# One stream of NF4 chunks through the attention steps, value scaling on ScalarE, and loads and stores moved between queues

## The chip, the cores and the metric

The kernel runs on one core of a Trainium2 chip. The metric is the device time of one execution in microseconds (us); lower is better. Engine names in the profile: PE is TensorE (PEld its weight loads), DVE is VectorE, ACT is ScalarE, POOL is GpSimd, SP is SyncE, whose queue issues the DMAs.

## The reference, cut to what matters

```python
# 8 batches x 128 tokens x 512; 32 query heads in 8 key/value groups of 4, head size 128; hidden 1376
h  = layernorm(x)
q, k, v = h @ Wq, ctx @ Wk, ctx @ Wv ; q, k = rope(q), rope(k)
logits  = 30 * tanh(q k^T * 0.0884 / 30), masked ; weights = softmax(logits)
x = x + (weights @ v) @ Wo
d1, d2, d3 = nf4(w1), nf4(w2), nf4(w3)   # blocks of 64: divide by absmax, take the nearest of
                                         # 16 codes (15 thresholds), multiply by absmax again
h = layernorm(x)
x = x + (silu(h @ d1^T) * (h @ d2^T)) @ d3^T
```

## The kernel before, in words

Each engine has its own instruction list, written by hand and executed strictly in its order; engines meet only through semaphores (`wait_ge(name, value)`). Matrices are split into a high and a low part so that three matmuls in fp32r give about fp32 accuracy; ScalarE makes the high part, VectorE or GpSimd the low one.

- **Start** (to about 160 us): pieces of weights and context are loaded, K is projected in 16 units with rope, V in 16 units `v`, x is normalised, and the first six query units (of 64) are projected in between.
- **The 64 steps.** Step j = 8*kv + b (group kv, batch b) has one list per engine. TensorE: `weighted_values(j)`, query projection `q_unit(j+6)`, `logits(j+2)`, `transpose4` of `nrm` for j, `out_unit(j-1)` (projection with Wo). VectorE: `add_out(j-2)`, the reciprocal of the softmax sums `rs` (L1026), the scaling of the values into `nrm` (L1029), NF4 additions, `rope_parts(j+6)` (L898, reads the projection), the last NF4 addition, the low part `atl` of j (L1048). ScalarE: one NF4 comparison, `high` (a weight piece, L720), `weights(j+2)` (tanh L763, exp L765), the high part `ath` of j (L780), the remaining NF4 comparisons. GpSimd: low parts of weight pieces, `mask(j+2)` (L1215), `query_rope(j+6)` (L1149, after two DMAs `swap` that exchange halves through `sw`), and NF4 `nf_normalise` and `nf_rescale` (L1165).
- **NF4.** The weights w1, w2, w3 come as 12 chunks of 128 x 1408 (chunk 0 and 9 to 11 from w3). For one chunk: load, `nf_prepare` (absmax of blocks, L871 and two small ones), `nf_normalise`, then 15 pairs of a comparison on ScalarE (`nf_above_bound`, L702, into the two slots of `nfp`) and an addition on VectorE (`nf_add`, L887 and L890), then `nf_rescale` and a store to a scratch in memory. Chunk 0 is done in the start (15 pairs over v = 0 to 12), chunks 1 to 8 in the 64 steps, one for each group of 8 steps (mostly 2 pairs a step), chunks 9 to 11 in the feed-forward part.
- **Feed-forward** (from about 690 us): 22 hidden units, each 24 matmuls; then the 11 pieces of w3 are transposed and split, and the down projection runs to the end.

In VectorE's list, a step's additions are divided in this way, with `bounds` the list of the step's thresholds:

```python
before = max(1, len(bounds) - 1)
for i in bounds[:before]: nf_add(kv + 1, i)
...rope_parts...
for i in bounds[before:]: nf_add(kv + 1, i)
dve.wait_ge(at_hi, j + 1)            # then atl of step j
```

Of the kernel before, what the change touches and what calls it, by code (L numbers as in the profile page):

```python
# [5 lines left out]
B, S, D = 8, 128, 512  # L6
# [35 lines left out]
def build(nc, x_d, ctx_t, wk_d, wv_d, wq_d, wo_d, nf_d, mask_t, table_d, out_d):  # L42
# [5 lines left out]
    with ctx:  # L48
# [71 lines left out]
        with ExitStack() as loop:  # L120
            cs_loop = sb("cs_loop", [128, 2, 2, 512], f32, loop)
            nfx = sb("nfx", [128, CH], f32, loop)
# [67 lines left out]
        def nf_bufs(c):  # L190

            if c == 0:
                return nfv, nfa
            if c > NKV:
                return [(nfa, nfy), (nfv, nfa), (nfy, nfv)][c - NKV - 1]
            return NF_BUF[(2 * c - 4) % 3], NF_BUF[(2 * c - 3) % 3]
# [45 lines left out]
        def nf_values(v):  # L242

            return range(15 * v // 13, 15 * (v + 1) // 13) if v < 13 else range(0)
# [9 lines left out]
        def nf_head(kv, b):  # L254

            if kv == NKV - 1:
                return [[0, 1], [2, 3], [4, 5, 6], [7, 8], [9, 10], [11], [12], [13, 14]][b]
            return [[0, 1], [2, 3], [4, 5], [6, 7], [8, 9], [10, 11], [12], [13, 14]][b]
# [11 lines left out]
        def _(sp):  # L270
# [17 lines left out]
            def nf_load(c):  # L288
                if c == 1 or c == NKV + 1:
                    sp.wait_ge(nf_above, 15 * c)  # L290
                elif c > 1:
                    sp.wait_ge(nf_out, nf_stored(c - 2))
                sp.dma_start(nf_bufs(c)[0][:, :], nf_d[:, c * CH:(c + 1) * CH]).then_inc(nf_in, 16)
# [36 lines left out]
            sp.dma_start(y[:, :, :], x_d.rearrange("b s d -> s b d")).then_inc(x_in, 16)  # L330
            nf_load(0)
# [42 lines left out]
            def head(kv):  # L374
                last = kv == NKV - 1
                j = 8 * kv
                head_piece(j + 3)
                if kv > 0:
                    wait(sp, av_done, j)
                    sp.dma_start(vcur[:, 4:8, 0:DH], vs_d[kv, 1]).then_inc(v_in[1], 16)  # L380
                if kv > 0:
                    nf_store(kv)
                query_swap(j + AHEAD)
                head_piece(j + 4)
                query_swap(j + AHEAD + 1)
                if not last:
                    nf_load(kv + 2)
                if not last:
                    wait(sp, logits_done, j + 4)
                    sp.dma_start(kcur[:, 0, :], ks_d[kv + 1, 0]).then_inc(k_in[0], 16)  # L390
                head_piece(j + 5)
                query_swap(j + AHEAD + 2)
                head_piece(j + 6)
                query_swap(j + AHEAD + 3)
                head_piece(j + 7)
                if not last:
                    wait(sp, av_done, j + 4)
                    sp.dma_start(vcur[:, 0:4, 0:DH], vs_d[kv + 1, 0]).then_inc(v_in[0], 16)
                query_swap(j + AHEAD + 4)
                head_piece(j + 8)  # L400
                query_swap(j + AHEAD + 5)
                if not last:
                    wait(sp, logits_done, j + 8)
                    sp.dma_start(kcur[:, 1, :], ks_d[kv + 1, 1]).then_inc(k_in[1], 16)
                head_piece(j + 9)
                query_swap(j + AHEAD + 6)
                head_piece(j + 10)
                query_swap(j + AHEAD + 7)
                if last:
                    sp.wait_ge(nf_out, nf_stored(NKV - 1))  # L410
                    for n in range(4):
                        weights_in(n)
                    nf_load(NKV + 1)
# [15 lines left out]
            nf_store(NKV)  # L429
# [3 lines left out]
            nf_load(NKV + 2)  # L433
            for n in range(4, 2 * HT):
                if n == 15:
                    nf_store(NKV + 1)
                if n == 17:
                    nf_load(NKV + 3)
                weights_in(n)
            w3v = dq3[:, 0:4 * HID].rearrange("p (i h) -> p i h", i=4)  # L440
            for n in range(HT):
                m = 2 * HT + n
                cols = 128 if n < HT - 1 else HLAST
                if n in (2, 7):
                    nf_store(NKV + 2 + n // 7)
# [12 lines left out]
        def _(pe):  # L458
# [76 lines left out]

            for v in range(16):
# [10 lines left out]
                if u is not None:  # L547
                    pe.wait_ge(xt_lo, 8)
                    q_unit(u)

            def logits(j):

                kv, h, s = j // B, j % B // 4, j % 4
                if s == 0:
                    pe.wait_ge(roped, NK + 8 * kv + 4 * h + 4)
                    pe.wait_ge(k_in[h], 16 * kv + 16)
                wait(pe, tanh_done, j)
                nc.tensor.matmul(lgp[:, :], kcur[:, h, s * 128:(s + 1) * 128],  # L558
                                 qT[:, h, :, s * 128:(s + 1) * 128], start=True, stop=True).then_inc(logits_done, 1)
# [59 lines left out]
            logits(0)  # L619
# [75 lines left out]
        def _(act):  # L695
# [43 lines left out]
            for n in range(16):  # L739
                first_hi(n)  # L740
            for u in range(10, NK):
# [25 lines left out]
            def head(kv):  # L767
                last = kv == NKV - 1
                for b in range(B):
                    j = 8 * kv + b  # L770
                    bounds = nf_head(kv, b)
                    for i in bounds[0:1]:
                        nf_above_bound(kv + 1, i)
# [7 lines left out]
                    for i in bounds[1:]:  # L781
                        nf_above_bound(kv + 1, i)
# [9 lines left out]
            def weight_hi(n):  # L792
                act.wait_ge(wt_done, n + 1)
                if n >= 4:
# [29 lines left out]
            for n in range(len(UNITS)):  # L824
# [13 lines left out]
                for c, i in nf_ffn(n):  # L838
                    nf_above_bound(NKV + 1 + c, i)
            hidden_hi(2 * HT - 1)  # L840
            for c, i in nf_ffn(2 * HT):
                nf_above_bound(NKV + 1 + c, i)
# [12 lines left out]
        def _(dve):  # L855
# [22 lines left out]
            def nf_add(c, i):  # L878
# [3 lines left out]
                if i == 0:  # L882
                    if c == 1:
                        dve.wait_ge(vproj_done, 16)
                    if c == NKV + 1:
# [125 lines left out]
            nf_prepare(1)  # L1011
# [6 lines left out]
            def head(kv):  # L1018
                last = kv == NKV - 1
                for b in range(B):  # L1020
                    j = 8 * kv + b
                    if j > 1:
# [5 lines left out]
                    dve.wait_ge(recip_done, j + 1)  # L1028
                    nc.vector.tensor_tensor(  # L1029
                        nrm[:, b % 2, :].rearrange("p (a c d) -> p a c d", a=2, c=2),  # L1030
                        avp[:, :, 0:2 * (DH + 1)].rearrange("p a (c d) -> p a c d", c=2)[:, :, :, 0:DH],
                        rs[:, :].rearrange("p (a c o) -> p a c o", a=2, c=2).to_broadcast([128, 2, 2, DH]),
                        ALU.mult).then_inc(an_done, 1)

                    bounds = nf_head(kv, b)
                    before = max(1, len(bounds) - 1)
                    for i in bounds[:before]:
                        nf_add(kv + 1, i)
                    if b == 6 and not last:
                        nf_prepare(kv + 2)  # L1040
# [3 lines left out]
                    for i in bounds[before:]:  # L1044
# [252 lines left out]
```

## Time and profile before

| | |
|---|---|
| Time, median of 3 runs | 920.55 us (914.53 to 921.25) |
| The profiled execution: its own time | 916.73 us |
| Its span in the profile | 914.8 us |
| Mean granted TensorE clock | 0.962 of full speed |
| Busy: PE, DVE, ACT, POOL | 89%, 73%, 51%, 49% |

A row of the timeline reads: start in us, duration in us, engine, line, operation, output<-input with sizes, count, and in brackets the time for which the engine was idle before it and who released it. Neighbouring instructions of one engine overlap slightly in the record, so the distance from start to start is what counts in a sum.

### The profile page before, as it was taken

The page shows a single profiled execution, that of the slowest core. Times are in us where ns is not written, and L with a number is a line of the kernel's source. Part 1 is how long each engine was busy: PE and PEld are TensorE (multiplying, and loading weights), DVE is VectorE, ACT ScalarE, POOL GpSimd, SP SyncE. Part 2 cuts the span into 40 slices and gives each one's busy share as a digit, 9 for nine tenths or more (in the row PEclk, how much of TensorE's full clock was granted, in tenths as well). Part 3 has the DMA queues.
Part 4 walks back from the last instruction along what each step waited for, and adds up shares of the span by engine and source line. Part 5 has one row for each costly group of instructions (what it writes and reads, how often), then busy time and mean ns, then how long its engine had stood idle before and what let it go on. Part 6 is the DMA issues. An engine that isn't in the chain of part 4 may idle for free.

```text
span 914.8 us, 10681 instructions
## 1 busy us (share of the span) xinstructions
PE 818.3 (89%) x3806; PEld 650.5 (71%) x3806; DVE 669.7 (73%) x743; ACT 466.7 (51%) x571; POOL 446.3 (49%) x272
## 2 busy tenths in 40 slices
PE   6688893999999999999998998997779797994998
PEld 4576782677788777777886776775567686883886
DVE  3777752788888898888887987888766589698120
ACT  4014742565565656555655655655332576677100
POOL 1645056556857758659659568474102223253000
PEclk9899997999999999999999999999799999998999
DMA  9564735333433423435325234213013013120210
GB/s 328 151 188 140 209 92 169 90 81 93 144 92 90 126 79 114 123 81 155 81 70 167 58 92 144 57 48 101 1 32 133 24 35 114 32 76 23 84 58 35
DMA packets 63540, 91.75 MB, mean 100 GB/s; under 512 B 6784, under 2 KB 30464, under 8 KB 63488
## 3 DMA queue, kind: packets, MB, share of 16 engines
q1 hardware_dynamic: 63488, 91.07, 34.1%
q8 instruction: 31, 0.51, 0.2%
q14 instruction: 21, 0.17, 0.1%
HBM read 51.00 MB, written 19.07 MB: 77 GB/s over the span
## 4 chain that ended last, share of the span: by engine, by line
PE 51%; POOL 15%; DVE 13%; DMA 8%; issue 6%; ACT 5%; SPq 2%; POOLq 0%; DVEq 0%; ACTq 0%
POOL qT L1149 6%; PE bank L463 5%; PE bank L465 4%; PE bank L464 4%; DMA sw<-cs_loop 4%; PE bank L558 4%; PE bank L497 3%; PE bank L499 3%; PE bank L498 3%; PE bank L481 3%; PE bank L482 3%; PE bank L483 3%; PE avp L569 3%; DMA sw<-cs_start 3%; PE trp L470 2%
## 5 line engine op out<-in xcount | busy, mean ns | idle before, releaser
L1149 POOL TENSOR_TENSOR qT<-cs_loop,sw 128x512 f32<-128x512 f32 x58 | 92.6, 1597 | 104.9 <-DMA sw<-cs_loop 99.8
L763 ACT ACTIVATE eb<-bank 128x512 f32<-128x512 f32 x64 | 38.3, 598 | 194.4 <-PE bank L558 194.4
L890 DVE SCALAR_TENSOR_TENSOR nfa<-nfp,nfa 128x1408 f32<-128x1408 uint8 x56 | 106.8, 1907 | 32.5 <-ACT nfp L702 31.2
L890 DVE SCALAR_TENSOR_TENSOR nfv<-nfp,nfv 128x1408 f32<-128x1408 uint8 x56 | 106.5, 1902 | 28.0 <-ACT nfp L702 26.8
L1215 POOL TENSOR_TENSOR eb<-eb,maskf 128x512 f32<-128x512 f32 x64 | 91.1, 1425 | 62.4 <-ACT eb L765 62.4
L702 ACT ACTIVATE nfp<-nfv,bnd 128x1408 uint8<-128x1408 f32 x75 | 107.0, 1460 | 20.4 <-POOL nfv L1165 15.8
L497 PE MATMUL bank<-woh,ath 128*128 128x512 f32 x256 | 109.4, 427 | 0.0
L481 PE MATMUL bank<-xh,wqh 128*128 128x512 f32 x256 | 106.5, 416 | 0.0
L499 PE MATMUL bank<-woh,atl 128*128 128x512 f32 x256 | 103.2, 403 | 0.0
L498 PE MATMUL bank<-wol,ath 128*128 128x512 f32 x256 | 103.0, 402 | 0.0
L890 DVE SCALAR_TENSOR_TENSOR nfx<-nfp,nfx 128x1408 f32<-128x1408 uint8 x42 | 79.9, 1902 | 30.2 <-ACT nfp L702 30.2
L483 PE MATMUL bank<-xh,wql 128*128 128x512 f32 x256 | 101.5, 397 | 0.0
L482 PE MATMUL bank<-xl,wqh 128*128 128x512 f32 x256 | 101.5, 396 | 0.0
L702 ACT ACTIVATE nfp<-nfa,bnd 128x1408 uint8<-128x1408 f32 x60 | 85.2, 1460 | 8.6 <-POOL nfa L1165 5.6
L1250 POOL TENSOR_TENSOR hl<-hf,hh 128x512 fp32r<-128x512 f32 x22 | 33.8, 1536 | 96.7 <-ACT hh L812 96.7
L569 PEld LDWEIGHTS avp<-vcur,eb 128*128 128x128 f32 x512 | 67.3, 193 | 18.9 <-POOL eb L1215 14.4
L569 PE MATMUL avp<-vcur,eb 128*128 128x129 f32 x512 | 68.4, 277 | 13.6 <-POOL eb L1215 13.6
L558 PE MATMUL bank<-qT,kcur 128*128 128x512 f32 x128 | 66.4, 600 | 13.2 <-POOL qT L1149 12.5
L470 PEld LDWEIGHTS trp<-tab,nrm 128*128 128x128 f32 x288 | 35.3, 144 | 57.2 <-DVE nrm L1029 31.5
L898 DVE TENSOR_TENSOR cs_loop<-bank,csq 128x1024 f32<-128x1024 f32 x58 | 69.9, 1206 | 2.0 <-PE bank L483 2.0
L463 PE MATMUL bank<-xh,wgh 128*128 128x512 f32 x176 | 71.2, 404 | 0.0
L464 PE MATMUL bank<-xl,wgh 128*128 128x512 f32 x176 | 69.8, 397 | 0.0
(134 smaller groups left out, 1814.4 us busy)
## 6 DMA issues: line engine op xcount, KB each, us to landing
sw<-cs_loop SPq DMA_DIRECT2D x116, 128.0 KB, 2.3
stage<-wq_pieces SPq DMA_DIRECT2D x32, 256.0 KB, 2.9
stage<-wo_pieces SPq DMA_DIRECT2D x32, 256.0 KB, 2.9
stage<-dq_scratch SPq DMA_DIRECT2D x32, 256.0 KB, 3.2
sw<-cs_start SPq DMA_DIRECT2D x44, 128.0 KB, 2.4
ks_scratch<-qT SPq DMA_DIRECT2D x16, 256.0 KB, 2.3
vs_scratch<-vst SPq DMA_DIRECT2D x16, 256.0 KB, 3.3
kcur<-ks_scratch SPq DMA_DIRECT2D x16, 256.0 KB, 3.2
```

The source lines that it names most:

```text
L463: nc.tensor.matmul(out, wh, mh, start=i == 0, stop=False)
L464: nc.tensor.matmul(out, wh, ml, start=False, stop=False)
L481: nc.tensor.matmul(o, wqh[:, g, k, :], xh[:, k, cs], start=k == 0, stop=False)
L482: nc.tensor.matmul(o, wqh[:, g, k, :], xl[:, k, cs], start=False, stop=False)
L483: last = nc.tensor.matmul(o, wql[:, g, k, :], xh[:, k, cs], start=False, stop=k == KT - 1)
L497: nc.tensor.matmul(o, ah, wh[:, g, :], start=g == 0, stop=False)
L498: nc.tensor.matmul(o, ah, wl[:, g, :], start=False, stop=False)
L499: last = nc.tensor.matmul(o, al, wh[:, g, :], start=False, stop=g == G - 1)
L569: av = nc.tensor.matmul(avp[:, g // 2, (g % 2) * (DH + 1):(g % 2 + 1) * (DH + 1)], eb[:, b % 2, g * 128:(g + 1) * 128], vcur[:, b, :], sta ...
L702: nc.scalar.activation(nfp[:, n % 2, :], nf_bufs(c)[0][:, :], ACT.Sign, bias=bnd[:, i:i + 1])\
L890: op = nc.vector.scalar_tensor_tensor(acc[:, :], nfp[:, n % 2, :], STEPS[i], acc[:, :], ALU.mult, ALU.add)
L1149: nc.gpsimd.tensor_tensor(dst, products(ru, slot)[:, 0, :], sw[:, slot, :], ALU.add).then_inc(roped, 1)
```

## The change

- The chunks 1 to 9 form one stream of positions, 16 for a chunk (15 pairs and, at the 13th position, the preparation of the next chunk). Steps 0 to 55 take 33 positions per 14 steps, steps 56 to 63 take 12 in 8. So a step has 1, 2 or 3 pairs. Chunk 9 moves from the feed-forward part into the steps; chunks 10 and 11 stay there, at 2 positions for each hidden unit, from unit 1 to unit 16. The buffers of the chunks are renamed accordingly.
- The scaling of the values into `nrm` leaves VectorE and becomes four ScalarE activations (one per head, 128 columns each, scale from `rs`). They stand first in ScalarE's list of a step, behind a wait for this step's reciprocal.
- x is loaded from ScalarE's queue after its 10th piece, chunk 0 after its 16th. Chunk 0's 15 pairs are spread over v = 0 to 10.
- `nf_store(0)` moves behind the last exchange of the start; in the steps, stores and loads of chunks stand behind the exchanges; SyncE's list of a step is written as a loop. `logits(0)` moves ahead of the sixth query unit; GpSimd normalises chunk 1 and masks step 0 ahead of its sixth rope.

```diff
         def nf_values(v):
-            return range(15 * v // 13, 15 * (v + 1) // 13) if v < 13 else range(0)
+            return range(15 * v // 11, 15 * (v + 1) // 11) if v < 11 else range(0)
+        def nf_sequence(lo, hi, first):
+            steps = [(first + p // 16, p % 16) for p in range(lo, hi)]
+            adds = [(c, r if r < 12 else r - 1) for c, r in steps if r != 12]
+            return adds, [c + 1 for c, r in steps if r == 12], [c for c, r in steps if r == 15]
+        def nf_head(j):
+            lo, hi = [33 * i // 14 if i <= 56 else 132 + 12 * (i - 56) // 8 for i in (j, j + 1)]
+            return nf_sequence(lo, hi, 1) if 0 <= j < NSTEP else ([], [], [])
         def nf_ffn(n):
-            return [divmod(k, 15) for k in range(45 * (n - 2) // 21, 45 * (n - 1) // 21)] if n >= 2 else []
+            lo, hi = [2 * (i - 1) for i in (n, n + 1)]
+            return nf_sequence(max(0, lo), min(hi, 32), NKV + 2)
@@ sync, start @@
-            sp.dma_start(y[:, :, :], x_d.rearrange("b s d -> s b d")).then_inc(x_in, 16)
-            nf_load(0)
...
-                if v == 13:
+                if v == 12:
                     nf_load(1)
-                if v == 14:
-                    nf_store(0)
...
+            nf_store(0)
             for i in range(4):
                 wait(sp, v_out[i], 64)
@@ sync, feed-forward @@
             for n in range(4, 2 * HT):
-                if n == 15:
-                    nf_store(NKV + 1)
-                if n == 17:
+                if n == 6:
                     nf_load(NKV + 3)
+                if n == 18:
+                    nf_store(NKV + 2)
                 weights_in(n)
@@ tensor, start @@
                 if u is not None:
                     pe.wait_ge(xt_lo, 8)
+                    if v == 15:
+                        logits(0)
                     q_unit(u)
@@ scalar, start @@
             for n in range(16):
                 first_hi(n)
+                if n == 9:
+                    act.dma_start(y[:, :, :], x_d.rearrange("b s d -> s b d")).then_inc(x_in, 16)
+            act.dma_start(nfv[:, :], nf_d[:, 0:CH]).then_inc(nf_in, 16)
@@ scalar, a step @@
-                    bounds = nf_head(kv, b)
-                    for i in bounds[0:1]:
-                        nf_above_bound(kv + 1, i)
+                    act.wait_ge(recip_done, j + 1)
+                    for g in range(G):
+                        col = (g % 2) * (DH + 1)
+                        last_part = nc.scalar.activation(nrm[:, b % 2, g * DH:(g + 1) * DH],
+                                                         avp[:, g // 2, col:col + DH], ACT.Copy, scale=rs[:, g:g + 1])
+                    last_part.then_inc(an_done, 1)
+                    adds = nf_head(j)[0]
+                    for c, i in adds[0:1]:
+                        nf_above_bound(c, i)
                     if not last:
                         high(32 + j)
...
                     nc.scalar.activation(ath[:, j % 4, :], trp[:, :], ACT.Copy).then_inc(at_hi, 1)
-                    for i in bounds[1:]:
-                        nf_above_bound(kv + 1, i)
+                    for c, i in adds[1:]:
+                        nf_above_bound(c, i)
@@ vector, a step @@
-                    dve.wait_ge(recip_done, j + 1)
-                    nc.vector.tensor_tensor(
-                        nrm[:, b % 2, :].rearrange("p (a c d) -> p a c d", a=2, c=2),
-                        avp[:, :, 0:2 * (DH + 1)].rearrange("p a (c d) -> p a c d", c=2)[:, :, :, 0:DH],
-                        rs[:, :].rearrange("p (a c o) -> p a c o", a=2, c=2).to_broadcast([128, 2, 2, DH]),
-                        ALU.mult).then_inc(an_done, 1)
-
-                    bounds = nf_head(kv, b)
-                    before = max(1, len(bounds) - 1)
-                    for i in bounds[:before]:
-                        nf_add(kv + 1, i)
-                    if b == 6 and not last:
-                        nf_prepare(kv + 2)
+                    adds, prepares, _ = nf_head(j)
+                    before = max(1, len(adds) - 1)
+                    for c, i in adds[:before]:
+                        nf_add(c, i)
+                    for c in prepares:
+                        nf_prepare(c)
                     u = j + AHEAD
                     if u < NUNIT:
                         rope_parts(NK + u, u % 2, csq[:, :, :])
-                    for i in bounds[before:]:
-                        nf_add(kv + 1, i)
+                    for c, i in adds[before:]:
+                        nf_add(c, i)
@@ gpsimd, start @@
+            for u in range(AHEAD):
+                if u == 5:
+                    nf_normalise(1)
+                    mask(0)
+                query_rope(u)
+                if u in (1, 3):
+                    for n in (28 + u - 1, 29 + u - 1):
+                        low(n % 4, woh0[:, n % 4, :], wol0[:, n % 4, :], n)
+                if u == 1:
+                    nf_rescale(0)
+            mask(1)
```

## Rows read from the trace of the kernel before

**Rows 1.** The page, part 1: busy us, share of the span, instructions, by engine.

```profile
PE 818.3 (89%) x3806; PEld 650.5 (71%) x3806; DVE 669.7 (73%) x743; ACT 466.7 (51%) x571; POOL 446.3 (49%) x272
```

**Rows 2.** Stage table, 250 to 300 us: busy PE, PEld, DVE, ACT, POOL; clock.

```profile
250.00:300.00 50.00, 49.96 (x244) 39.33 (x243) 42.99 (x49) 30.21 (x39) 32.43 (x20) 1.00 0.34 94
```

**Rows 3.** Timeline of VectorE, step 55, up to the reciprocal of step 56.

```profile
603.19 0.17 DVE L1026 RECIPROCAL rs<-avp 128x4 f32<-128x4 f32 x1
...
605.54 1.22 DVE L898 TENSOR_TENSOR cs_loop<-bank,csq 128x1024 f32<-128x1024 f32 x1
608.82 1.94 DVE L890 SCALAR_TENSOR_TENSOR nfx<-nfp,nfx 128x1408 f32<-128x1408 uint8 x1 [2.07 <-ACT nfp L702]
610.68 0.68 DVE L1048 TENSOR_TENSOR atl<-trp,ath 128x512 fp32r<-128x512 f32 x1
...
611.88 0.17 DVE L1026 RECIPROCAL rs<-avp 128x4 f32<-128x4 f32 x1
```

**Rows 4.** Timeline of ScalarE in the same step.

```profile
605.68 0.60 ACT L763 ACTIVATE eb<-bank 128x512 f32<-128x512 f32 x1 [4.10 <-PE bank L558]
...
607.33 1.46 ACT L702 ACTIVATE nfp<-nfv,bnd 128x1408 uint8<-128x1408 f32 x1
```

**Rows 5.** Timeline of ScalarE in step 1, its list without gaps.

```profile
166.96 2.82 ACT L702 ACTIVATE nfp<-nfv,bnd 128x1408 uint8<-128x1408 f32 x2
169.68 0.62 ACT L720 ACTIVATE wqh<-stage 128x512 fp32r<-128x512 f32 x1
170.30 0.60 ACT L763 ACTIVATE eb<-bank 128x512 f32<-128x512 f32 x1
```

**Rows 6.** Timeline of VectorE, step 58, the only one with three pairs.

```profile
627.60 0.17 DVE L1026 RECIPROCAL rs<-avp 128x4 f32<-128x4 f32 x1
...
632.39 3.35 DVE L890 SCALAR_TENSOR_TENSOR nfv<-nfp,nfv 128x1408 f32<-128x1408 uint8 x2 [2.37 <-ACT nfp L702]
...
636.87 0.17 DVE L1026 RECIPROCAL rs<-avp 128x4 f32<-128x4 f32 x1
```

**Rows 7.** Groups by line and form: busy us, mean ns, idle before.

```profile
L720 ACT ACTIVATE wqh<-stage 128x512 fp32r<-128x512 f32 x28 | 17.3, 619 | 0.0
...
L1029 DVE TENSOR_TENSOR nrm<-avp,rs 128x512 f32<-128x512 f32 x64 | 44.2, 691 | 2.2
...
L890 DVE SCALAR_TENSOR_TENSOR nfx<-nfp,nfx 128x1408 f32<-128x1408 uint8 x42 | 79.9, 1902 | 30.2 <-ACT nfp L702 30.2
```

**Rows 8.** Timeline of VectorE: preparation of a chunk, to the next instruction.

```profile
745.82 1.61 DVE L871 TENSOR_REDUCE nfm<-nfv 128x22 f32<-128x1408 f32 x1
...
747.89 3.29 DVE L890 SCALAR_TENSOR_TENSOR nfy<-nfp,nfy 128x1408 f32<-128x1408 uint8 x2
```

**Rows 9.** Timeline of VectorE, reciprocal of step 0.

```profile
160.75 0.18 DVE L1026 RECIPROCAL rs<-avp 128x4 f32<-128x4 f32 x1 [14.30 <-PE avp L569]
```

**Rows 10.** Timelines of GpSimd and of SyncE's queue, end of the start.

```profile
139.81 1.28 POOL L1149 TENSOR_TENSOR qT<-cs_start,sw 128x512 f32<-128x512 f32 x1 [3.52 <-DMA sw<-cs_start]
141.05 2.53 POOL L1140 TENSOR_TENSOR wol<-stage,woh 128x512 fp32r<-128x512 f32 x2
...
146.11 0.88 SPq L303 DMA_DIRECT2D dq_scratch<-nfa  x2
...
154.80 2.55 POOL L1165 TENSOR_TENSOR nfv<-nfv,nfr 128x1408 f32<-128x1408 f32 x1
157.31 2.49 POOL L1215 TENSOR_TENSOR eb<-eb,maskf 128x512 f32<-128x512 f32 x2
```

**Rows 11.** Timeline of TensorE, a K unit of the start after a wait.

```profile
27.85 0.77 PE L523 MATMUL bank<-cth,wch 128*128 128x512 f32 x1 [5.60 <-DVE cs_start L898]
```

**Rows 12.** TensorE's waits in the feed-forward part: us in total, times, longest.

```profile
PE bank L671 <- DVE w3l L1125: 11.7, 1, 11.7
PE bank L470 <- DMA stage<-dq_scratch: 5.0, 1, 5.0
PE trp L470 <- DVE wgl L1072: 4.9, 1, 4.9
```

More of the change, by code:

```diff
@@ L375, in head @@
                 last = kv == NKV - 1
[L376 to L413, printed above, removed]
+                for b in range(B):
+                    j = 8 * kv + b
+                    head_piece(j + 3)
+                    if b == 0 and kv > 0:
+                        wait(sp, av_done, j)
+                        sp.dma_start(vcur[:, 4:8, 0:DH], vs_d[kv, 1]).then_inc(v_in[1], 16)
+                    if b == 4 and not last:
+                        wait(sp, av_done, j)
+                        sp.dma_start(vcur[:, 0:4, 0:DH], vs_d[kv + 1, 0]).then_inc(v_in[0], 16)
+                    query_swap(j + AHEAD)
+                    if b in (1, 5) and not last:
+                        wait(sp, logits_done, j + 3)
+                        sp.dma_start(kcur[:, b // 4, :], ks_d[kv + 1, b // 4]).then_inc(k_in[b // 4], 16)
+                    for c in nf_head(j - 2)[2]:
+                        nf_store(c)
+                    for c in nf_head(j - 3)[2]:
+                        nf_load(c + 2)
+                    if j == 1:
+                        nf_load(2)
+                    if last and b == 3:
+                        sp.wait_ge(nf_out, nf_stored(NKV - 1))
+                        for n in range(4):
+                            weights_in(n)
@@ L534, in _, with logits @@
                     first_transposes(u - 10)
+            def logits(j):
+                kv, h, s = j // B, j % B // 4, j % 4
+                if s == 0:
+                    pe.wait_ge(roped, NK + 8 * kv + 4 * h + 4)
+                    pe.wait_ge(k_in[h], 16 * kv + 16)
+                wait(pe, tanh_done, j)
+                nc.tensor.matmul(lgp[:, :], kcur[:, h, s * 128:(s + 1) * 128],
+                                 qT[:, h, :, s * 128:(s + 1) * 128], start=True, stop=True).then_inc(logits_done, 1)
             for v in range(16):
@@ L1112, in _ @@
                 hidden(n)
-                if n in (1, 7, 14):
-                    nf_prepare(NKV + 1 + n // 7)
-                for c, i in nf_ffn(n):
-                    nf_add(NKV + 1 + c, i)
-            for c, i in nf_ffn(2 * HT):
-                nf_add(NKV + 1 + c, i)
+                adds, prepares, _ = nf_ffn(n)
+                for c in prepares:
+                    if c < 12:
+                        nf_prepare(c)
+                for c, i in adds:
+                    nf_add(c, i)
             for n in range(HT):
@@ L1200, in query_rope @@
                 rope(NK + u, u % 2, qT[:, half, g, :])
-            for u in range(AHEAD):
-                query_rope(u)
-                if u in (1, 3):
-                    for n in (28 + u - 1, 29 + u - 1):
-                        low(n % 4, woh0[:, n % 4, :], wol0[:, n % 4, :], n)
-                if u == 3:
-                    nf_rescale(0)
-            nf_normalise(1)
             def mask(j):
@@ L1222, in head @@
                     j, slot = 8 * kv + b, b % 4
-                    if b == 7 and not last:
-                        nf_normalise(kv + 2)
-                    if b == 0 and kv > 0:
-                        nf_rescale(kv)
+                    for c in nf_head(j - 1)[2]:
+                        nf_rescale(c)
                     if not last and b < 4:
@@ L1234, in head @@
                         query_rope(j + AHEAD)
+                    for c in nf_head(j)[1]:
+                        nf_normalise(c)
                     if last and b == 4:
@@ L1238, in head @@
                         power(2, range(2, 4))
-            mask(0)
-            mask(1)
             for kv in range(NKV):
```

57 lines of the change are left out of this document (22 added, 35 removed).

## The prediction

> **What bounds the kernel now.** I read the page's busy shares first: TensorE is busy for 89% of the span, VectorE for 73%, ScalarE for 51% [rows 1]. By these numbers ScalarE has room for more work. But a share is a mean over stages, so I went to the table of stages: in a 50 us stretch of the 64 steps TensorE is busy for 49.96 us, VectorE for 42.99, ScalarE for 30.21 [rows 2]. From the reciprocal of step 0 at 160.75 [rows 9] to that of step 56 at 611.88 [rows 3] are 451.1 us, 8.06 us a step. TensorE is the bound there, with VectorE a little below it.
>
> Then I looked at which wait ends last for VectorE within a step, because its list and ScalarE's refer to each other. In step 55 the reciprocal starts at 603.19, the last NF4 addition at 608.82 after 2.07 us of waiting for ScalarE's comparison, `atl` follows 1.86 us later, and 1.20 us after that (`atl` and `add_out`, 0.60 each) the next reciprocal [rows 3]. ScalarE started its tanh at 605.68, released by TensorE's logits, and the comparison that VectorE waited for at 607.33 [rows 4]. So before the change the chain inside a step starts at TensorE: logits, tanh, exp, `ath`, comparison, addition, `atl`, `add_out`, reciprocal. Nothing in ScalarE's list waits for the reciprocal itself; it depends on it only through TensorE's transposes.
>
> **The steps: a closed ring between two engines.** The change puts the four scaling activations at the head of ScalarE's step, behind a wait for the reciprocal. Queued behind that wait are a comparison, `high`, tanh, exp, `ath` and the other comparisons; VectorE waits for the last of these before its last addition, and only then come `atl`, `add_out` and the next reciprocal. That is a ring: reciprocal of j, ScalarE's step up to the comparison that the last addition needs, the end of VectorE's step, reciprocal of j+1. No buffer loosens it, since both lists are in order. Its length, start to start:
> - reciprocal to ScalarE: 0.17 and 0.03 of handing over (comparison at 607.33 ends at 608.79, addition starts at 608.82 [rows 3, 4]): 0.20.
> - four activations of 128 columns. No row shows one that narrow. The comparison over 1408 columns takes 1.46 [rows 4], the copy over 512 takes 0.62 [rows 7]: 0.94 ns a column and 0.14 fixed, so 0.26 each, 1.05 for four. Bounds: 0.5 (the columns alone) and 1.9 (each at about the 0.48 by which a 512-wide one advances its engine, if the fixed part of one that reads PSUM and a scale were as large as that). I take 1.05, as both rows lie on that line.
> - first comparison: two in a row take 2.82, so 1.36; `high` to tanh 0.62 [rows 5].
> - tanh to the last addition's start: 608.82 - 605.68 = 3.14 [rows 3, 4].
> - addition to `atl`: 1.86 in step 55; two additions in a row take 3.35 in step 58, so 1.6 at least [rows 3, 6], 1.54 with the overlap; the mean duration is 1.90 [rows 7].
> - `atl` and `add_out`: 1.20.
>
> For a step with two pairs: 0.20+1.05+1.36+0.62+3.14 = 6.37 to the last addition, then 1.54 to 1.86, then 1.20: 9.1 to 9.4 us. A check: in step 55 the same addition started 5.63 after the reciprocal, and the step took 8.69; 0.74 later gives 9.43.
>
> For three pairs VectorE does two before `rope_parts`, and the second of these needs a comparison that ScalarE makes behind `ath`. So `rope_parts` (1.14 [rows 3]) and one more addition go onto the ring: 11.8 to 12.4. Step 58, the one with three pairs now, took 9.27 without rope, its second addition starting at 4.79 [rows 6]; 6.37 - 4.79 + 1.14 later is 12.0.
>
> The preparation of a chunk (2.07 [rows 8]) lies between the first addition and `rope_parts`. First addition at 2.74, then 1.54 to 1.86, 2.07, 1.14: 7.5 to 7.8, past the 6.37. With two pairs 10.2 to 10.9, with one 8.7 to 9.0.
>
> Steps 0 to 55 by the new rule: 33 with two pairs, 15 with three, 5 with two and a preparation, 3 with one and a preparation. The sum is 555 with the short additions and 579 with the long ones. The mean of the additions speaks for the long ones, less traffic of GpSimd for the short ones; I take 572, against 451: +121. What VectorE sheds (0.69 a step [rows 7]) does not shorten the ring; it is replaced by 1.05 on ScalarE plus 1.36 and 0.62 which were beside it before. TensorE needs 8.06 a step and waits for the scaled values; its projections still run beside the ring.
>
> Steps 56 to 63: they have 11 additions where there were 15, 7.6 us less by the mean, no `high`, and the first steps of the feed-forward part between them, which were already serial. Against it stand the ring in the three steps with two pairs and the preparation in step 61. I put the difference at 0, with 6 either way.
>
> The Trainium skill, ScalarE: Activation LUTs, section What ACT_TABLE_LOAD costs, gives 280 ns + 0.833 ns a column for an activation with one pointer operand, and an overlap of 93 ns; the comparison here agrees (1453 against 1460 ns), and four of 128 columns would come to about 1.27 by it, an estimate that adds 12 us over 56 steps. The same page, section Rules for kernel authors, sends multiplications to VectorE; by the rows here the move costs 1.05 against 0.69 in busy time alone, and the ring is worth much more than that.
>
> **The start.** x and chunk 0 leave SyncE's queue, where the first exchange stood behind them. TensorE waited 5.60 us at 27.85 for that [rows 11]; I count 4 of it as gained (0 to 6, since the same 16 DMA engines carry x either way). Issuing the two DMAs costs ScalarE 0 to 2 us, hidden as its next work then is the first transpose of x, long after. Chunk 0's pairs in 11 instead of 13 steps `v` put about one pair more on a ScalarE that TensorE already waits for there: 1 us lost (0 to 3).
>
> At the end of the start GpSimd's last rope came late, as its exchange was queued behind the store at 146.11, which waited for the rescaling; then came the normalisation at 154.80 and the mask at 157.31 [rows 10], and TensorE began the steps. Now: rope 3 at 139.81 to 141.1, two low parts (2.5), rope 4 (1.3), normalisation (2.5), first mask (1.3) end at 148.7 instead of 158.6: 9.9 gained. All of the start: -13, between -18 and -7. The logits ahead of the sixth query unit cost TensorE up to a microsecond of waiting for rope 3, within that.
>
> **The feed-forward part.** Three waits of TensorE [rows 12]. 4.9 us: the low parts of weights stood behind an addition that waited for chunk 9's normalisation; that chunk is now done in the steps and chunk 10 is prepared there. 5.0: a weight piece behind a store in SyncE's queue; the store now comes at n = 18, when its data have long been ready. 11.7: the splitting of w3 behind the last additions; these end at unit 16 of 22, and a serial transpose, high and low part of about 2.5 remain. Gain 19, and about 1 for the slow clock after the waits (the matmul after the 5.60 us wait takes 0.77 [rows 11], and its line's mean is about half of that): -20, bounds -14 and -26.
>
> **Sum.** 914.8 - 13 + 121 + 0 - 20 = 1003 of span; with the 1.9 that lie around it (916.73 - 914.8) 1005. That execution is 0.4% under the median of 920.55, which is no more than the runs spread; I leave it so.
>
> **The rivals.**
> - Faster: the sum of loads decides and the ring does not bind. VectorE's 6.9 us a step (42.99/50 x 8.06 [rows 2]) stay 6.8 (0.69 less, and 2.2 additions instead of 1.9), ScalarE's 4.9 become 6.4 (1.05, and 0.3 comparisons), TensorE stays the bound, and the better placed exchanges save some 5 us of its waits. 914.8 - 13 - 20 - 5 + 1.9 = 879. It holds if ScalarE's wait for the reciprocal ends less than about 2 us after TensorE's values, so early that the ring is under 8.06. Against it: the ring's members are all rows, in list order, and even its shortest form with activations of 0.5 us gives 8.6. 8%.
> - About the same: the ring binds only in the steps with three pairs, which costs 15 x 4 = 60 less what short steps give back, so that it nearly pays for the gains: 915 to 945. For it: steps with one pair are shorter than TensorE's work. Against it: there are 3 of these in 56. 5%.
> - Much slower, by the clock: TensorE waits 1 to 4 us in each step, and falls to the lower of its levels (1.2 of 2.4 GHz) as it did at 27.85 [rows 11]. At the lower level for half of the time its step would be 8.06 x 1.5 = 12.1, more than the ring, 678 for 56 steps: 1110. Against it: its chain from the reciprocal to the next values skips the query projection, so that it can lose 1 to 2 us a step unseen. 7%.
> - Slower by dear activations: 1.9 for four puts 0.85 on 64 steps: 1059. 10%.
> - The forecast: 70%.
>
> The range: from cheap activations and short additions (-29 and -17, start and end at their good bounds -11, not all at once) to dear ones: 960 to 1050. A measurement of this kernel tells about 1% from no change. Faster by more: 8%, with a little of the second rival 9%; within 1%: 2%; slower: 89%.
>
> **What would show it.** Right: the distance of reciprocals is 9 to 9.5 in most steps and about 12 in those with three pairs; ScalarE's idle time stands before the first scaling activation, released by VectorE's reciprocal, about 3 us a step; TensorE's transposes wait for `nrm` from ScalarE in nearly every step; the mask of step 0 ends near 149; no wait of over 4 us in TensorE's feed-forward part. Wrong: TensorE busy for over 95% between 200 and 600 us, or its clock there under 0.9.

## The result and the profile after

The changed kernel takes 1009.79 us (median of 4 runs, 1007.07 to 1011.64) against 917.54 for the kernel before: 1.100 times, interval 1.094 to 1.1065. It is 10% slower. The forecast was 1005 in 960 to 1050.

Busy shares, from the page of the kernel after (compare [rows 1]):

```profile
PE 857.4 (85%) x3806; PEld 671.8 (67%) x3806; DVE 629.0 (62%) x679; ACT 532.4 (53%) x827; POOL 444.4 (44%) x272
```

No engine is over 85%, and none of the other three is over 62%. A table of loads finds no bound here. The stage table, of the same columns as [rows 2], says it again for a stretch of the steps:

```profile
300.00:350.00 50.00, 43.57 (x200) 33.94 (x199) 32.86 (x32) 31.19 (x52) 24.37 (x16) 0.94 0.34 93
```

What ended the idle times does find it. The waits of ScalarE and of VectorE over the whole span, in the kernel after:

```profile
ACT nrm L765 <- DVE rs L1024: 242.2, 64, 5.7
```

```profile
DVE nfa L887 <- ACT nfp L690: 73.8, 40, 2.6
DVE nfv L887 <- ACT nfp L690: 71.6, 38, 2.6
DVE nfx L887 <- ACT nfp L690: 69.8, 35, 5.2
```

ScalarE waits 242 us for the reciprocal, in each of the 64 steps, and VectorE 215 us for ScalarE's comparisons. Two engines that wait for each other in step after step, while both are busy for less than two thirds of the time, look like a ring; the experiments below test it. The timeline of VectorE in one step with two pairs and one with three (compare [rows 3] and [rows 6]; L1024 is the reciprocal, L895 `rope_parts`, L1040 `atl`, L1013 `add_out`):

```profile
306.74 0.17 DVE L1024 RECIPROCAL rs<-avp 128x4 f32<-128x4 f32 x1
309.47 1.63 DVE L887 SCALAR_TENSOR_TENSOR nfa<-nfp,nfa 128x1408 f32<-128x1408 uint8 x1 [2.56 <-ACT nfp L690]
311.01 1.22 DVE L895 TENSOR_TENSOR cs_loop<-bank,csq 128x1024 f32<-128x1024 f32 x1
312.98 2.00 DVE L887 SCALAR_TENSOR_TENSOR nfa<-nfp,nfa 128x1408 f32<-128x1408 uint8 x1 [0.75 <-ACT nfp L690]
314.91 0.68 DVE L1040 TENSOR_TENSOR atl<-trp,ath 128x512 fp32r<-128x512 f32 x1
...
316.11 0.17 DVE L1024 RECIPROCAL rs<-avp 128x4 f32<-128x4 f32 x1
...
322.35 1.99 DVE L887 SCALAR_TENSOR_TENSOR nfa<-nfp,nfa 128x1408 f32<-128x1408 uint8 x1 [1.89 <-ACT nfp L690]
324.27 1.21 DVE L895 TENSOR_TENSOR cs_loop<-bank,csq 128x1024 f32<-128x1024 f32 x1
325.40 1.61 DVE L887 SCALAR_TENSOR_TENSOR nfa<-nfp,nfa 128x1408 f32<-128x1408 uint8 x1
...
328.13 0.17 DVE L1024 RECIPROCAL rs<-avp 128x4 f32<-128x4 f32 x1
```

And ScalarE in the first of these steps (compare [rows 4, 5]; L765 scaling, L690 comparison, L708 `high`, L754 tanh, L756 exp, L777 `ath`):

```profile
306.94 1.14 ACT L765 ACTIVATE nrm<-avp,rs 128x128 f32<-128x128 f32 x4 [3.93 <-DVE rs L1024]
307.95 1.48 ACT L690 ACTIVATE nfp<-nfx,bnd 128x1408 uint8<-128x1408 f32 x1
309.31 0.64 ACT L708 ACTIVATE woh<-stage 128x512 fp32r<-128x512 f32 x1
309.83 0.61 ACT L754 ACTIVATE eb<-bank 128x512 f32<-128x512 f32 x1
310.48 0.63 ACT L756 ACTIVATE eb<-eb 128x512 f32<-128x512 f32 x1
311.01 0.58 ACT L777 ACTIVATE ath<-trp 128x512 fp32r<-128x512 f32 x1
311.49 1.46 ACT L690 ACTIVATE nfp<-nfx,bnd 128x1408 uint8<-128x1408 f32 x1
```

Read it from 306.74: reciprocal, at 306.94 ScalarE wakes, runs through its list without one gap, at 312.98 VectorE's last addition can start, and at 316.11 comes the next reciprocal: 9.37 us. In the second step `rope_parts` has come to stand between two additions: 12.02 us.

The reciprocals of steps 0 and 56, at 160.75 and 611.88 before, are now at 148.15 and 730.37. So the start gained 12.6 us, steps 0 to 55 lost 131.1 (582.2 against 451.1), and the rest, 302.9 before and 278.5 now, gained 24.4. Their sum, +94.1, is the difference of the spans (1008.9 - 914.8).

### The profile page after: what moved, and what is told of

The parts are those of the page before. It is cut to its first block, busy times and chain, and to the rows that moved or that the text cites. A ratio compares the mean times of both kernels' runs of the same rounds, so it can differ in the third digit from the quotient of the medians.

```text
span 1008.9 us, 10873 instructions
## 1 busy us (share of the span) xinstructions
PE 857.4 (85%) x3806; PEld 671.8 (67%) x3806; DVE 629.0 (62%) x679; ACT 532.4 (53%) x827; POOL 444.4 (44%) x272
## 4 chain that ended last, share of the span: by engine, by line
PE 32%; ACT 24%; DVE 22%; issue 15%; DMA 4%; POOL 2%; SPq 1%; ACTq 0%; POOLq 0%; DVEq 0%
ACT nfp L690 13%; ACT nrm L765 5%; PE bank L450 4%; PE bank L452 4%; PE bank L451 4%; DVE nfa L887 4%; DVE y L1013 3%; DVE nfx L887 3%; DVE nfv L887 3%; ACT ath L777 2%; ACT eb L754 2%; PE bank L659 2%; PE bank L660 2%; PE bank L661 2%; DVE cs_loop L895 2%
## 5 line engine op out<-in xcount | busy, mean ns | idle before, releaser
L765 ACT ACTIVATE nrm<-avp,rs 128x128 f32<-128x128 f32 x256 | 73.0, 368 | 242.2 <-DVE rs L1024 242.2
L887 DVE SCALAR_TENSOR_TENSOR nfa<-nfp,nfa 128x1408 f32<-128x1408 uint8 x56 | 101.8, 1818 | 74.5 <-ACT nfp L690 73.8
L1141 POOL TENSOR_TENSOR qT<-cs_loop,sw 128x512 f32<-128x512 f32 x58 | 74.0, 1276 | 164.0 <-DMA sw<-cs_loop 164.0
L484 PE MATMUL bank<-woh,ath 128*128 128x512 f32 x256 | 123.2, 481 | 0.0
L457 PE MATMUL trp<-tab,nrm 128*128 128x128 f32 x288 | 53.6, 317 | 79.9 <-ACT nrm L765 79.7
L485 PE MATMUL bank<-wol,ath 128*128 128x512 f32 x256 | 114.3, 446 | 0.0
L486 PE MATMUL bank<-woh,atl 128*128 128x512 f32 x256 | 112.9, 441 | 0.0
L690 ACT ACTIVATE nfp<-nfv,bnd 128x1408 uint8<-128x1408 f32 x75 | 108.6, 1466 | 3.8 <-POOL nfv L1157 3.0
L530 PE MATMUL bank<-qT,kcur 128*128 128x512 f32 x128 | 72.4, 649 | 35.4 <-POOL qT L1141 35.2
L1132 POOL TENSOR_TENSOR wol<-stage,woh 128x512 fp32r<-128x512 f32 x32 | 70.5, 2207 | 41.6 <-ACT woh L708 41.6
L1132 POOL TENSOR_TENSOR wql<-stage,wqh 128x512 fp32r<-128x512 f32 x28 | 62.3, 2225 | 59.2 <-ACT wqh L708 59.2
L690 ACT ACTIVATE nfp<-nfa,bnd 128x1408 uint8<-128x1408 f32 x60 | 86.9, 1467 | 1.2 <-POOL nfa L1157 1.0
L895 DVE TENSOR_TENSOR cs_loop<-bank,csq 128x1024 f32<-128x1024 f32 x58 | 70.0, 1207 | 0.0
```

What stands on the lines that cost most here:

```text
L457: last = nc.tensor.transpose(out[0:p, i * 128:(i + 1) * 128], src(i), tab[:, 2, :])
L484: nc.tensor.matmul(o, ah, wh[:, g, :], start=g == 0, stop=False)
L485: nc.tensor.matmul(o, ah, wl[:, g, :], start=False, stop=False)
L486: last = nc.tensor.matmul(o, al, wh[:, g, :], start=False, stop=g == G - 1)
L690: nc.scalar.activation(nfp[:, n % 2, :], nf_bufs(c)[0][:, :], ACT.Sign, bias=bnd[:, i:i + 1])\
L765: last_part = nc.scalar.activation(nrm[:, b % 2, g * DH:(g + 1) * DH], avp[:, g // 2, col:col + DH], ACT.Copy, scale=rs[:, g:g + 1])
```

## The experiments

Each run is compared with the kernel before, measured again beside it (medians of 916 to 918). The first ones ask whether it is the ring, and whether its members have the prices that the forecast gave them.

**The scaling back on VectorE.** Everything else of the change stays. The first hunk is ScalarE's step, the second VectorE's, behind the reciprocal.

```diff
@@ scalar @@
-                    act.wait_ge(recip_done, j + 1)
-...
@@ vector @@
+                    dve.wait_ge(recip_done, j + 1)
+                    nc.vector.tensor_tensor(
+...
+                        ALU.mult).then_inc(an_done, 1)
```

> The changed kernel with the scaling of the values back on VectorE as one instruction behind the reciprocal; all else of the change stays. Ring theory: ScalarE's list no longer waits for the reciprocal, the steps with two pairs fall from 9.7 back to about 8.1 us, those with three from 12.0 to about 10, with a preparation to about 8.8; 56 steps in about 485 to 500 instead of 582, time 910 to 930. Load theory (the slowdown comes from more work on ScalarE and lower TensorE clock in proportion): VectorE is given 44 us more, ScalarE 73 less, time 990 to 1010. Chunk theory (the ninth chunk in the steps is what costs): no change, about 1009.

Measured: 935.6 us, ratio to before 1.020 (1.017 to 1.023). 74 of the 92 us are gone with the ring, though VectorE is given work and its busy time rises from 629 to 674. The load theory and the theory that the ninth chunk alone is the cost fall. It is 6 us above the range: steps with three pairs take 11.2, not 10, and the 56 steps 513 where 485 to 500 were expected and the kernel before takes 451. So the rest of the change, the stream of chunks above all, has a price of its own in the steps, with no ring between the two engines.

**The scaling on ScalarE, but third in its list.** The same instructions, in another order.

```diff
+                    adds = nf_head(j)[0]
+                    for c, i in adds[0:1]:
+                        nf_above_bound(c, i)
+                    if not last:
+                        high(32 + j)
                     act.wait_ge(recip_done, j + 1)
...
-                    adds = nf_head(j)[0]
-                    for c, i in adds[0:1]:
-                        nf_above_bound(c, i)
-                    if not last:
-                        high(32 + j)
```

> The changed kernel with the same instructions, but in ScalarE's list of a step the wait for the reciprocal and the four scaling activations stand behind the first comparison and the copy high, ahead of tanh. Ring theory: these two (1.36 + 0.52) leave the ring, which is then 0.20+1.05+3.14+1.86+1.20 = 7.4 us for two pairs, below TensorE's 8.06, and 10.3 for three; 56 steps in 490 to 510, time 915 to 940. Load theory: the work of each engine is unchanged, so about 1009. Chunk theory: about 1009.

Measured: 944.6 us, 1.029 (1.022 to 1.035). No engine's work changed and 65 us went, by order alone. The range is missed by 5 us: the steps with three pairs take 11.2 and not 10.3, the ones with two 8.6 in the mean, 7.95 in the median.

**One member off the ring.**

```diff
-                    if not last:
-                        high(32 + j)
                     if j + 2 < NSTEP:
                         weights(j + 2)
...
                     for c, i in adds[1:]:
                         nf_above_bound(c, i)
+                    if not last:
+                        high(32 + j)
```

> The changed kernel with only the copy high moved behind the last comparison of a step. Ring theory: 0.52 us leave the ring in 56 steps, -29 us, time 975 to 985, unless the later low parts on GpSimd delay the rope (then up to 1000). Load theory and chunk theory: about 1009.

Measured: 984.2 us, 1.074 (1.070 to 1.077), 25.5 less than the changed kernel. The copy advances ScalarE by 0.52 (309.31 to 309.83 above), 29 us in 56 steps, and the 56 steps fell by 23.4, from 582.2 to 558.8. The price of 0.52 is not seen by itself in every kind of step. The median step with two pairs fell by 0.89, from 9.36 to 8.47, since the last addition got shorter too; start to start to `atl` it is 1.54 here and was 1.93 above (312.98 to 314.91):

```profile
300.59 1.63 DVE L887 SCALAR_TENSOR_TENSOR nfa<-nfp,nfa 128x1408 f32<-128x1408 uint8 x1 [0.23 <-ACT nfp L690]
302.13 0.68 DVE L1040 TENSOR_TENSOR atl<-trp,ath 128x512 fp32r<-128x512 f32 x1
```

Step 0 fell by 4.1, while the steps with three pairs kept their mean of 12.06 (their median fell by 0.47). So the sum comes near the forecast in part by balance.

**The scaling alone, on the kernel before.** The activations head ScalarE's step, and VectorE's multiplication into nrm is taken out.

```diff
+                    act.wait_ge(recip_done, j + 1)
+...
                     bounds = nf_head(kv, b)
```

> The kernel before with one part of the change alone: the four scaling activations at the head of ScalarE's step behind the wait for the reciprocal, instead of VectorE's instruction. Ring theory: the steps of two pairs take 9.3 to 9.5 instead of 8.06, 56 steps in about 525 instead of 451, time 985 to 1000. Load theory: VectorE sheds 44 us and ScalarE stays under 65% busy, about 917 or less. Chunk theory: no change, 917.

Measured: 1000.6 us, 1.091 (1.087 to 1.095), 0.6 above the range. With 1.9 pairs a step and none of the new chunk stream, 56 steps take 527.5 (451.1 before). Every one is nearly alike: reciprocal to reciprocal 9.29 to 9.75. So this one edit carries most of the loss. The rest of the change adds 9 us on top of it. That is a balance and not nothing: in the spans these 56 steps get 55 us longer with the chunk stream in them (582.2 against 527.5), and the start gives back 12 and the part behind step 56 another 32.

**`rope_parts` off the ring,** in the steps with three pairs.

```diff
-                    before = max(1, len(adds) - 1)
+                    before = 1
```

> The changed kernel with VectorE doing only the first addition of a step ahead of rope_parts (so in steps with three pairs the second one comes behind it). Ring theory: in these 15 steps rope_parts (1.14) leaves the ring, 12.0 falls to 10.9, -17 us, and with exchanges that start 3 us earlier TensorE's logits wait less; 990 to 995. The rival that the steps with three pairs cost because of VectorE's load: no change, about 1009.

Measured: 992.9 us, 1.083 (1.080 to 1.086). Timeline of VectorE in such a step of this run:

```profile
308.00 0.17 DVE L1024 RECIPROCAL rs<-avp 128x4 f32<-128x4 f32 x1
...
312.27 1.22 DVE L895 TENSOR_TENSOR cs_loop<-bank,csq 128x1024 f32<-128x1024 f32 x1
314.24 3.73 DVE L887 SCALAR_TENSOR_TENSOR nfa<-nfp,nfa 128x1408 f32<-128x1408 uint8 x2 [0.75 <-ACT nfp L690]
...
319.09 0.17 DVE L1024 RECIPROCAL rs<-avp 128x4 f32<-128x4 f32 x1
```

11.09 where it was 12.02: `rope_parts` now lies in VectorE's wait for the comparison. The 1.13 by which it advances VectorE are gone, and the two additions behind it take 0.2 more than in the changed kernel. So `rope_parts` was on the ring at the price that the term for three pairs gave it.

**The same edit with the scaling on VectorE** (x1 and x5 together).

> The run with the scaling back on VectorE, and rope_parts ahead of the second addition as in x5. Without the ring the open chain from TensorE's logits over ScalarE to the last additions still holds in steps with three pairs (11.2 there). Chain theory: rope_parts leaves it, 11.2 falls to about 9.8, 56 steps from 513 to about 492, time 912 to 918. Load theory (VectorE now has 2.2 additions and the scaling, 7.6 us a step): the time stays at 935.

Measured: 911.9 us, 0.996 (0.993 to 1.000), at the lower end of the range. 24 us less than x1; steps with three pairs 10.1, 56 steps in 490.9. This is as fast as the kernel before, with one chunk more in the steps: the start and the feed-forward part now pay for the loop.

**Two comparisons ahead.** With the scaling on VectorE (the first run) and with it on ScalarE behind the two comparisons and `high` (the second). Both also have the edit of x5, `before = 1`.

```diff
-                    for c, i in adds[0:1]:
+                    for c, i in adds[0:2]:
                         nf_above_bound(c, i)
...
-                    for c, i in adds[1:]:
+                    for c, i in adds[2:]:
                         nf_above_bound(c, i)
```

> As x6 (scaling on VectorE), and ScalarE does two comparisons of a step ahead of high and tanh, where it waits for logits anyway. Chain theory: in steps with two pairs nothing of NF4 lies behind ath, in those with three only one pair; VectorE's own 7.6 us and TensorE's 8.06 decide, 56 steps in 455 to 470 instead of 513, time 875 to 895. Load theory: 935.

> As x8, but with the scaling on ScalarE as in x2: two comparisons, high, then the wait for the reciprocal and the four activations, then tanh. The ring is 0.20+1.05+0.63+0.54+0.60+1.20 = 4.2 for two pairs and about 8 for three, so TensorE decides; VectorE has 6.8 us a step instead of 7.6. Chain theory: 56 steps in 450 to 465, time 870 to 890, at or below x8. Rival: the move to ScalarE is bad by itself (four activations of 1.05 against 0.69): 10 us or more above x8.

Measured: 891.7 us, 0.973 (0.9705 to 0.975), and 891.9, 0.9725 (0.970 to 0.975). Both beat both kernels. 56 steps took 476 and 473 us, 6 and 8 over the forecasts, and the second run's time is 2 us above its range. The move to ScalarE is not bad by itself: tanh, exp and `ath` still wait behind it, but the ring that is left, 4.2 us for two pairs by the expectation, is far below TensorE's step, and the two runs are alike. In the second, two steps took over 14 us. ScalarE's timeline in one of them:

```profile
307.27 1.46 ACT L690 ACTIVATE nfp<-nfx,bnd 128x1408 uint8<-128x1408 f32 x1
315.74 1.47 ACT L690 ACTIVATE nfp<-nfv,bnd 128x1408 uint8<-128x1408 f32 x1 [7.00 <-POOL nfv L1157]
317.11 0.61 ACT L708 ACTIVATE woh<-stage 128x512 fp32r<-128x512 f32 x1
317.63 1.12 ACT L770 ACTIVATE nrm<-avp,rs 128x128 f32<-128x128 f32 x4
```

The comparison that was drawn forward is the first of a new chunk; it waits for GpSimd's normalisation, with the scaling, tanh and exp queued behind it. It is the fault of the change again, in small.

**Not across a chunk's start.** For both places of the scaling, on top of the last two runs.

```diff
+                    ahead = 1 if len(adds) > 1 and adds[1][1] == 0 else 2
-                    for c, i in adds[0:2]:
+                    for c, i in adds[0:ahead]:
                         nf_above_bound(c, i)
...
-                    for c, i in adds[2:]:
+                    for c, i in adds[ahead:]:
                         nf_above_bound(c, i)
```

> As x9, but where the second comparison of a step is the first of a new chunk, ScalarE does it behind ath again and not ahead of tanh. In x9 two of the steps of this kind (20 and 54) took 14.3 and 14.2 us. Chain theory: ScalarE stood there waiting for GpSimd's normalisation with tanh and the scaling queued behind it; they fall to about 8, 10 to 13 us in all, time 878 to 883. Rival: the long steps come from somewhere else (a late weight piece or rope), then 890 as x9.

> As x8 (scaling on VectorE) with the same edit. Its steps of this kind took 10.4 and 10.0, so about 2 us each are to be had: 886 to 890. If the scaling on ScalarE is worth its place once it is off the ring, because VectorE is next to the bound, x11 ends 5 us or more below this run; if the two engines are both covered by TensorE, within 2.

Measured: 885.6 us, 0.964 (0.959 to 0.970), and 886.6, 0.967 (0.962 to 0.9725). In the first run the two long steps fell from 14.3 and 14.2 to 9.2 and 8.9. In the second, where they were 10.4 and 10.0, they fell by 0.5 and 0.6 and not by the 2 expected, so they explain only 1 of the 5 us that it gained over x8. The time is 3 us above the forecast for the first. The difference of the two runs, 1 us, is within the bound set for "both covered". The better one is the fastest kernel of the study, 3.6% under the kernel before.

**Two comparisons ahead, on the kernel before.**

```diff
-                    for i in bounds[0:1]:
+                    for i in bounds[0:2]:
                         nf_above_bound(kv + 1, i)
...
-                    for i in bounds[1:]:
+                    for i in bounds[2:]:
                         nf_above_bound(kv + 1, i)
```

> The kernel before with one edit only: ScalarE does two comparisons of a step ahead of high and tanh. With 1.9 pairs a step TensorE was the bound there and VectorE waited 2 us a step for a comparison without harm. Chain theory: the loop stays at TensorE's 8.06, at best its waits for the rope (about 10 us) go: 907 to 917. Rival: what made x8 fast is the order of the comparisons alone, not the better start and feed-forward part: about 892.

Measured: 903.4 us, 0.986 (0.980 to 0.993), 4 us under the range of the chain theory and 11 above the rival's 892. The steps went from 451.1 to 443.4. The reciprocals come 7.74 apart in most of the steps (the median step of the kernel before took 7.75 already), and VectorE waits for TensorE at both ends of a step, as its timeline shows:

```profile
307.80 0.18 DVE L1026 RECIPROCAL rs<-avp 128x4 f32<-128x4 f32 x1 [0.20 <-PE avp L569]
...
314.65 0.69 DVE L1015 TENSOR_TENSOR y<-bank,y 128x512 f32<-128x512 f32 x1 [0.69 <-PE bank L499]
315.54 0.18 DVE L1026 RECIPROCAL rs<-avp 128x4 f32<-128x4 f32 x1 [0.20 <-PE avp L569]
```

So 7.74 is TensorE's own step (it was busy for 50.00 of the 50 us from 250 to 300), and the 8.06 that the prediction called TensorE's need was too high. Of the 0.32 between them this order took back 0.14; TensorE's waits for the rope, 9.3 us in 6 waits between 162 and 600, are most of the rest. Of what x11 gains over the kernel before (32 us), this order alone has 14. The rest is a balance: x11's start and its part behind step 56 are 10.5 and 26 us shorter than here, and its 56 steps, with the ninth chunk in them, 21 longer.

The steps 0 to 55 by kind, mean distance of the reciprocals in us, worked out from the timeline of each run's profiled execution (that of x2 took 936.0, 8.6 less than its median; the others are within 3.5 us of theirs):

| run | two pairs | three pairs | two, preparation | one, preparation | sum of 56 |
|---|---|---|---|---|---|
| before | 8.16 | | | 7.30 | 451.1 |
| forecast | 9.1 to 9.4 | 11.8 to 12.4 | 10.2 to 10.9 | 8.7 to 9.0 | 572 |
| after | 9.68 | 12.05 | 10.84 | 9.30 | 582.2 |
| x4, scaling alone | 9.44 | | | 9.30 | 527.5 |
| x3, high last | 9.11 | 12.06 | 10.20 | 8.72 | 558.8 |
| x5, rope first | 9.41 | 11.35 | 10.84 | 9.30 | 562.9 |
| x2, scaling third | 8.58 | 11.15 | 8.81 | 7.17 | 516.0 |
| x1, scaling back | 8.38 | 11.19 | 8.92 | 8.07 | 513.3 |
| x6 | 8.24 | 10.11 | 8.80 | 7.73 | 490.9 |
| x8 | 7.61 | 10.46 | 8.90 | 7.89 | 476.3 |
| x9 | 7.71 | 10.09 | 8.90 | 7.51 | 472.7 |
| x11 | 7.43 | 10.24 | 8.67 | 7.51 | 464.8 |
| x12 | 7.65 | 10.10 | 8.93 | 7.76 | 471.7 |
| x13 | 7.94 | | | 7.74 | 443.4 |

## Why the prediction was right, point by point

**The ring** was right in its mechanism (x1, x2: off the ring most of the loss goes, with the same work or more) and in its members (x3, x4, x5: `high` 0.52, the scaling with what it drags behind it 76 us on the kernel before, `rope_parts` 1.13). Their sizes were near and their errors offset each other. The four activations advance ScalarE by 1.01 us (306.94 to 307.95) where 1.05 was taken, `high` by 0.52 where 0.62 was, so that the last addition starts 6.24 after the reciprocal where 6.37 was; the addition itself takes 1.93 to `atl`, above the 1.54 to 1.86 of the forecast.

**The steps' sum** was 10 us short, 131 for 121. The median step with two pairs is 9.36, within its bounds; the mean of 9.68 is not. Most of the difference lies in seven of the 33 steps with two pairs. Step 0 took 13.0, as ScalarE waited for a weight piece whose load had moved behind the chunk's store:

```profile
154.44 0.63 ACT L708 ACTIVATE wqh<-stage 128x512 fp32r<-128x512 f32 x1 [3.57 <-DMA stage<-wq_pieces]
```

The load's place does that, and not the ring: in x1, without the ring, step 0 takes 12.7 with the same wait. The other six (6, 14, 26, 34, 42 and 54) took 9.7 to 11.4. Each stands behind a step with a late `rope_parts`, and is one in which TensorE's logits need that rope. They waited for it for 4 to 5.8 us, of which 0.6 to 1.3 came through to ScalarE's tanh. In TensorE's waits of the kernel after:

```profile
PE trp L457 <- ACT nrm L765: 79.7, 31, 5.8
PE bank L530 <- POOL qT L1141: 35.2, 10, 5.8
```

Before, the wait for the rope was 12.5 us. The prediction put `rope_parts` on the ring and did not ask who else was waiting for it. x5 agrees: its steps with two pairs fall from 9.68 to 9.41, though the edit does not touch them. Step 14, behind one with three pairs, fell from 11.38 to 9.01, and step 6, behind a preparation that x5 leaves as it was, stayed at 10.6; a quarter of the fall is its step 0, 10.8 for 13.0. The wait is not the whole of it, as longer additions beside GpSimd's normalisation take part too. This one is in step 6:

```profile
214.81 2.89 DVE L887 SCALAR_TENSOR_TENSOR nfx<-nfp,nfx 128x1408 f32<-128x1408 uint8 x1 [2.56 <-ACT nfp L690]
```

TensorE's transposes waited for `nrm` 31 times and their weight loads 46 times, not in nearly every one of the 64 steps as foreseen. ScalarE's wait for the reciprocal is 3.8 us a step where about 3 was.

**The start** was right in its sum, 12.6 for 13, and not in its parts. The mask of step 0 ends at 146.9, 11.7 us sooner, where 9.9 was worked out, since rope 3 itself came 3 us sooner, at 136.70 for 139.81; in SyncE's queue a chunk's load stood just ahead of its exchange before and does not now, which fits, though no run tests it. The exchanges that start sooner at the front of the kernel gave nothing in the end: TensorE's wait of 5.60 at 27.85 became two of 2 us, and `rope_parts` of the third K unit came 4.0 us sooner (22.47 for 26.48), but that of the eighth only 1.4 and that of the sixteenth 0.3. A wait for a context piece, before and after, stayed nearly as it was:

```profile
PE bank L523 <- DVE ctl L914: 6.3, 1, 6.3
PE bank L510 <- DVE ctl L911: 5.9, 1, 5.9
```

The 4 us counted there did not come through: the copy of the last V unit stands at 140.37 where it stood at 139.61. So the whole gain of the start was made behind that point, and that the sum of 13 came out is luck in these terms.

**The last eight steps and the feed-forward part** gained 24.4 for 20. Of TensorE's three waits [rows 12] that of 5.0 is gone, of that of 4.9 some 1.2 is left, and that of 11.7 is this:

```profile
PE bank L659 <- DVE w3l L1117: 2.4, 1, 2.4
```

2.5 had been left for it. The other 4 us are within the 6 given to steps 56 to 63; no run here parts them. In the sum of the forecast they stand against the 10 missed in the steps, which brings 1005 within 5 us of 1009.8.

**The rivals.** The sum of loads failed: no engine was full. "About the same" failed, as every kind of step got longer, those with one pair too (9.3). The clock did fall, from a mean of 0.962 to 0.932, and in stretches of 50 us between 200 and 750 it was 0.88 to 0.97; one of the two signs given for "wrong", a clock under 0.9, was touched in single stretches, while the mean of 200 to 600 is 0.92. In the typical step it was hidden as argued: x4, at a mean clock of 0.962, has a median of 9.37 in its steps with two pairs, and the changed kernel at 0.932 one of 9.36. What the lower clock cost in the longer steps no run parts. Dear activations failed by the 1.01.

## What to carry to other kernels

Before work is moved to the idler engine, write down who waits for what in both lists: a wait at the head of an in-order list puts everything behind it on the path of whatever the waited-for engine needs next. If that closes a ring, its length and not any engine's load is the step; here 9.4 us, where TensorE's own step was 7.7. The cure was order and not less work: what needs nothing goes ahead of the wait (two comparisons, `high`), what others need soonest goes first behind it. But nothing that may itself wait, like the first comparison of a new chunk, is drawn in front.

## What the runs showed of the hardware that was not expected

The group of the scaling activations in the page after gives 368 ns for one:

```profile
L765 ACT ACTIVATE nrm<-avp,rs 128x128 f32<-128x128 f32 x256 | 73.0, 368 | 242.2 <-DVE rs L1024 242.2
```

Yet four of them take 1.14 us in all, and the engine's next instruction starts 1.01 after the first, 0.25 each. About 0.11 of each lies beside the next. By the mean alone the four would have been put at 1.47. The Trainium skill, ScalarE: Activation LUTs, section What ACT_TABLE_LOAD costs, has 280 + 0.833 x 128 = 387 ns for one and an overlap of 93; the first is 5% above the row, the second a little under the 110 measured.

The same addition on VectorE has no single price. In the 64 steps of the kernel after, 25 of those that the timeline lists singly have no work of GpSimd beside them, and all 25 take 1.61 to 1.63 us. Of the 101 with GpSimd at work beside them, half take the same and 51 more than 1.7, up to 3.67. What in GpSimd's work makes the difference is not shown. The last addition of a typical step is a long one in the changed kernel and a short one in x3, 0.39 apart.
